# Adding the probabilities of two key blocks before the product with ones

## The reference, cut to what matters

```python
q = (xn @ Wq)  # 8 heads of 32;  k, v: 2 key heads, each shared by 4 query heads
scores = where(causal, rope(q) @ rope(k).T * scale, NEG);   out = softmax(scores) @ v
geo = where(causal, qp[:, None] * kp[None, :], NEG);         geo_out = softmax(geo) @ v
out = out + head_scales * (geo_out - out);   attention = out @ Wo
z = xn @ ternary(W_syn).T + b_syn;  keep the 102 largest of 1024 per row, relu
ffn = layernorm(xn + hidden @ ternary(W_out).T + b_out)
```

## Time and profile before

| | |
|---|---|
| median of 3 runs | 785.38 us (783.82 to 786.79) |
| the profiled execution | 785.15 us, of which the span is 783.4 us |
| mean granted TensorE clock | 0.896 |
| busy in the span | PE 703.4, DVE 495.6, ACT 464.9, POOL 262.5 us |

### The profile page before, as it was taken

How to read it: one execution, slowest core, us unless ns; L and a number is a source line. 1 busy time by engine, 2 the same in 40 slices (tenths; PEclk the granted TensorE clock), 3 DMA queues, 4 the chain that set the end, 5 groups by cost and what they waited for, 6 DMA issues and landing times. The chain is left out here.

```text
span 783.4 us, 12828 instructions
## 1 busy us (share of the span) xinstructions
PE 703.4 (90%) x4536; PEld 351.5 (45%) x4536; DVE 495.6 (63%) x1022; ACT 464.9 (59%) x789; POOL 262.5 (34%) x390
## 2 busy tenths in 40 slices
PE   2779889989999997999999997799999999989954
PEld 1445434455344344543344334544544455554434
DVE  3798498854675686266474648274575576856463
ACT  3354762058654611765554461688889888988930
POOL 5516562043214104331030102302433543343355
PEclk9876987589799975999999898899999999999986
DMA  8100000000000000000000000000000000000000
GB/s 234 63 1 4 7 2 7 0 3 1 1 8 1 1 1 2 1 5 6 1 1 1 1 2 1 10 1 8 8 8 8 8 8 15 8 8 8 2 0 28
DMA packets 12373, 9.41 MB, mean 12 GB/s; under 512 B 5713, under 2 KB 11729, under 8 KB 12306
## 3 DMA queue, kind: packets, MB, share of 16 engines
q1 hardware_dynamic: 12306, 8.55, 3.8%
HBM read 5.80 MB, written 2.10 MB: 10 GB/s over the span
## 5 line engine op out<-in xcount | busy, mean ns | idle before, releaser
L728 ACT ACTIVATE probs<-scores 128x1024 f32<-128x1024 f32 (+3 forms) x320 | 269.8, 893 | 153.9 <-PE acc L1208 56.3
L1208 PE MATMUL acc<-probs,v_nat 128*32 128x512 f32 (+3 forms) x1280 | 159.0, 570 | 6.1 <-POOL probs L606 5.8
L1208 PE MATMUL acc<-probs,ones_all 128*32 128x512 f32 (+3 forms) x1280 | 153.7, 553 | 0.0
L926 DVE TENSOR_REDUCE piece_max<-side 128x1 f32<-128x512 f32 x156 | 103.5, 686 | 73.9 <-PE side L1107 72.9
L606 POOL TENSOR_SCALAR_AFFINE_SELECT probs<-probs 128x256 f32<-128x256 f32 x128 | 57.9, 463 | 156.8 <-ACT probs L728 155.8
L1107 PE MATMUL side<-k_stack,q_stack 96*128 96x512 f32 (+3 forms) x232 | 93.5, 462 | 3.7 <-DVE piece_max L926 1.8
L1188 PE MATMUL scores<-q_stack,k_stack 98*128 98x512 f32 (+3 forms) x320 | 92.2, 398 | 2.4 <-ACT probs L728 2.4
L1208 PEld LDWEIGHTS acc<-probs,ones_all 128*32 128x32 f32 x1280 | 43.0, 115 | 82.9 <-issue 80.1
L1107 PEld LDWEIGHTS side<-k_stack,q_stack 96*128 96x128 f32 x232 | 42.1, 203 | 71.2 <-issue 45.6
L1188 PEld LDWEIGHTS scores<-q_stack,k_stack 98*128 98x128 f32 x320 | 55.3, 195 | 27.5 <-ACT probs L728 19.1
L641 POOL TENSOR_TENSOR xb<-xn,b_down 128x256 f32<-128x256 f32 x16 | 12.4, 776 | 147.8 <-DVE y_mv L1059 138.3
(11 more groups left out here) (144 smaller groups left out, 1105.9 us busy)
## 6 DMA issues: line engine op xcount, KB each, us to landing
res<-in_L_attn_x_dram SPq DMA_DIRECT2D x4, 512.0 KB, 9.2
out_dram<-res SPq DMA_DIRECT2D x16, 128.0 KB, 1.7
z_buf<-in_L_ffn_W_syn_dram SPq DMA_DIRECT2D x1, 1024.0 KB, 7.8
z_buf<-in_L_ffn_W_out_dram SPq DMA_DIRECT2D x1, 1024.0 KB, 4.9
k_geo<-geo_rows SPq DMA_DIRECT2D x24, 8.0 KB
q_geo<-geo_rows SPq DMA_DIRECT2D x24, 8.0 KB
w_qkv<-in_L_attn_Wq_dram SPq DMA_DIRECT2D x1, 256.0 KB, 4.4
tables<-in_cos_table_dram SPq DMA_DIRECT2D x1, 256.0 KB, 4.5
```

What stands on the lines that cost most here:

```text
L728: nc.scalar.activation(probs[:, slot % 2, pair, :, off:], scores[:, pair, :, off:], ACT.Exp, scale=ATT_SCALE if kind == 0 else 1.0).then_i ...
L926: free(nc.vector.tensor_reduce(piece_max[:, h, p:p + 1], pt, AX.X, ALU.max), ("S",) + a)
L1208: last = nc.tensor.matmul(acc[D * h:D * h + D, part, off:], lhs, probs[:, slot % 2, h // 2, h % 2, off:], start=first, stop=end)
```

## The change

1. The step `vs` is parted in two: `val` (the product with `v_nat`, every slot) and `sum` (the product with ones, every second slot).
2. Before a `sum`, the probabilities of the odd block j are added in place onto those of the even block j-1: pair 0 by DVE, pair 1 by POOL, one `tensor_tensor` of up to 128x1024 each (`add`). An add waits for `exp` (or `cut`) of its pair of block j and for `val` of block j-1. The columns that block j doesn't have stay as they were in j-1.
3. `probs` gets three buffers, and the planner chooses which one an `exp` takes: that of an even block is free after its `sum`, that of an odd block after its `val` and both adds.
4. Each copy after a pass waits only for its own half of `acc`, and each half of `acc` only for its own copy.
5. To make room, `z_buf` goes from three buffers to two (`z` of tile t waits for `hide` of t-2) and `q_geo` from two to one: `geo_dma` of chunk c now waits for the last `val` of chunk c-1. The bias row `b_up` moves from the third buffer of `z_buf` into `work`, so the first `pick` waits for the bias to be split.

```diff
-            wait = [("vs", c - 2, G - 1, 1, TPC * (c - 1) - 1)] if c >= 2 else []
+            wait = [("val", c - 2, G - 1, 1, TPC * (c - 1) - 1)] if c >= 2 else []
...
-            + ([("vs", c - 2, G - 1, 1, TPC * (c - 1) - 1)] if c >= 2 else []))
+            + ([("val", c - 1, G - 1, 1, TPC * c - 1)] if c >= 1 else []))
...
-                + ([("hide", t - 3)] if t >= 3 else [("w_put", 1, 3), ("b_split",)]), empties=("z", t, half))
+                + ([("hide", t - 2)] if t >= 2 else [("w_put", 1, 3), ("b_split",)]), empties=("z", t, half))
...
-        add("vs", "pe", 13, ("vs", c, g, kind, j), 60 + 1700 * share,
-            [("cut" if j >= TPC * c else "exp", c, g, kind, j, PAIRS - 1)]
-            + ([("o_raw",) + epilogues[e - 1], ("d_raw",) + epilogues[e - 1]] if j == 0 and e else []), "columns")
+        add("val", "pe", 13, ("val", c, g, kind, j), 60 + 850 * share,
+            [(made, c, g, kind, j, PAIRS - 1)] + ([("o_raw",) + epilogues[e - 1]] if j == 0 and e else []), "columns")
+        if j % 2:
+            for pair in range(PAIRS):
+                add("add", ADDERS[pair], 0, ("add", c, g, kind, j, pair), (150 + 2340 * share) / 2 if ADDERS[pair] == "dve" else 150 + 2500 * share,
+                    [(made, c, g, kind, j, pair), ("val", c, g, kind, j - 1)])
+            add("sum", "pe", 12.5, ("sum", c, g, kind, j), 60 + 850 * min(1, share + 1 / TPC * (j >= TPC * c)),
+                [("add", c, g, kind, j, pair) for pair in range(PAIRS)]
+                + ([("d_raw",) + epilogues[e - 1]] if j == 1 and e else []), "columns")
...
+    def kept_until(i):
+        if kept[i] is None:
+            return 0.0
+        c, g, kind, j = kept[i]
+        if j % 2 == 0:
+            users = [("sum", c, g, kind, j + 1)]
+        else:
+            users = [("val", c, g, kind, j)] + [("add", c, g, kind, j, pair) for pair in range(PAIRS)]
+        return max(done[u] for u in users) + HAND if all(u in done for u in users) else None
...
+                if k == "add":
+                    c, g, kind, j, pair = a
+                    off = max(0, j - TPC * c) * P
+                    if j >= TPC * c:
+                        dve.wait_ge(cut_ready, cut_no[a] + 1)
+                    else:
+                        dve.wait_ge(probs_ready, score_no[a] + 1)
+                    dve.wait_ge(vals_used, val_no[(c, g, kind, j - 1)] + 1)
+                    even, odd = (probs[:, buffer[(c, g, kind, i)], pair, :, off:] for i in (j - 1, j))
+                    nc.vector.tensor_tensor(even, even, odd, ALU.add).then_inc(added[pair], 1)
...
-                    for part, lhs in enumerate((v_nat[:, j, g], ones[:, 0:D])):
-                        for h in range(HG):
-                            last = nc.tensor.matmul(acc[D * h:D * h + D, part, off:], lhs,
-                                                    probs[:, slot % 2, h // 2, h % 2, off:], start=first, stop=end)
-                    last.then_inc(probs_used, 1)
+                    for h in range(HG):
+                        last = nc.tensor.matmul(acc[D * h:D * h + D, 0, off:], v_nat[:, j, g],
+                                                probs[:, buffer[a], h // 2, h % 2, off:], start=(j == 0), stop=(j == TPC * (c + 1) - 1))
+                    last.then_inc(vals_used, 1)
+                if k == "sum":
+                    c, g, kind, j = a
+                    e = epi_no[a[:3]]
+                    off = max(0, j - 1 - TPC * c) * P
+                    for i in range(PAIRS):
+                        pe.wait_ge(added[i], add_no[i][a] + 1)
+                    if j == 1 and e >= 1:
+                        pe.wait_ge(d_ready, e)
+                    for h in range(HG):
+                        last = nc.tensor.matmul(acc[D * h:D * h + D, 1, off:], ones[:, 0:D],
+                                                probs[:, buffer[(c, g, kind, j - 1)], h // 2, h % 2, off:],
+                                                start=(j == 1), stop=(j == TPC * (c + 1) - 1))
+                    last.then_inc(sums_used, 1)
```

More of the change, by code:

```diff
@@ L147, in build_plan @@
         share = 1 - max(0, j - TPC * c) / TPC
+        e = epilogues.index((c, g, kind))
+        made = "cut" if j >= TPC * c else "exp"
         for pair in range(PAIRS):
@@ L238, in build_plan @@
                 ready = max(ready, min(free_from(i) for i in spare))
+            if key[0] == "exp" and key[5] == 0:
+                spare = [kept_until(i) for i in range(BUFFERS) if kept_until(i) is not None]
+                if not spare:
+                    continue
+                ready = max(ready, min(spare))
             if key[0] == "score":
@@ L259, in build_plan @@
                     holds[BANKS + 2 * key[5] + i] = key
+        if key[0] == "exp" and key[5] == 0:
+            i = min((i for i in range(BUFFERS) if kept_until(i) is not None), key=kept_until)
+            earlier[key[1:5]], kept[i] = kept[i], key[1:5]
+            buffer[key[1:5]] = i
         clock[eng] = start + ns
@@ L426, in attention_and_ternary_ffn @@
         cut_ready = sem("cut_ready")
-        probs_used = sem("probs_used")
-        raw_ready = sem("raw_ready")
+        vals_used = sem("vals_used")
+        sums_used = sem("sums_used")
+        added = [sem(f"added{pair}") for pair in range(PAIRS)]
+        o_ready = sem("o_ready")
+        d_ready = sem("d_ready")
         recip_ready = sem("recip_ready")
@@ L722, in _ @@
                     off = max(0, j - TPC * c) * P
-                    slot = slot_no[(c, g, kind, j)]
                     act.wait_ge(score_full, n + 1)
-                    if pair == 0 and slot >= 2:
-                        act.wait_ge(probs_used, slot - 1)
-                    nc.scalar.activation(probs[:, slot % 2, pair, :, off:], scores[:, pair, :, off:], ACT.Exp,
+                    last = earlier[a[:4]]
+                    if pair == 0 and last and last[3] % 2 == 0:
+                        act.wait_ge(sums_used, sum_no[last[:3] + (last[3] + 1,)] + 1)
+                    if pair == 0 and last and last[3] % 2 == 1:
+                        act.wait_ge(vals_used, val_no[last] + 1)
+                        for i in range(PAIRS):
+                            act.wait_ge(added[i], add_no[i][last] + 1)
+                    nc.scalar.activation(probs[:, buffer[a[:4]], pair, :, off:], scores[:, pair, :, off:], ACT.Exp,
                                          scale=ATT_SCALE if kind == 0 else 1.0).then_inc(probs_ready, 1)
@@ L1192, in _ @@
                             last = nc.tensor.matmul(dst[:, off:], k_geo[rows, P * j:P * j + P],
-                                                    q_geo[rows, b, g, off:], start=True, stop=True)
+                                                    q_geo[rows, g, off:], start=True, stop=True)
                     last.then_inc(score_full, 1)
-                if k == "vs":
+                if k == "val":
                     c, g, kind, j = a
-                    slot, e = slot_no[a], epi_no[a[:3]]
+                    e = epi_no[a[:3]]
                     off = max(0, j - TPC * c) * P
-                    first, end = j == 0, j == TPC * (c + 1) - 1
                     if j >= TPC * c:
```

91 lines of the change are left out of this document (54 added, 37 removed).

## The result

The changed kernel takes 850.03 us (median of 4 runs, 847.88 to 876.3) where the kernel before takes 785.38: the ratio is 1.0815, with a 95% interval of 1.0782 to 1.0847. It is slower by 65 us, where 32 us of gain were forecast. The profiled execution has a span of 848.4 us.

A forecast was written before the change was run, and what follows sets the result against it. PE was taken to bound C and most of B, and D with ACT close behind; DVE set A's second half. Gains of 1 + 8.7 + 14.4 + 8 = 32 us from 785.15 gave 753 us, range 728 to 789.

The forecast's parts named there:

- the waits: PE waits 0.25 us per sum for adds: 2, 4, 6, 8 us in A to D; exp's buffer waits 0.
- the room: Fewer buffers: q_geo and the bias cost 0; for z_buf only 8 of the 17 us that ACT allows in D were taken.
- PE's time: Ones products removed take 66.0 us from PE: 5.1, 12.7, 20.4 and 27.8 in A to D.
- A: Stretch 58 to 165 us, from chunk 0's row-maxima transfer to chunk 1's; DVE ends it; gain put at 1 us.
- D: Stretch 492 to 760 us, from chunk 3's row-maxima transfer; ACT's limit 251 us; gain put at 8 us.
- B: Stretch 165 to 304 us, from chunk 1's row-maxima transfer to chunk 2's; gain put at 8.7 us.
- C: Stretch 304 to 492 us, from chunk 2's row-maxima transfer to chunk 3's; PE sets the pace; gain put at 14.4 us.
- the adds: A full add takes 1.25 us on DVE, 2.35 on POOL; neither engine passes its stretch, hidden beside PE in B, C, D.
- contention: DVE and POOL block each other when both read two operands from SBUF; cost put inside the 0.25 us per sum.
- the path shared by DVE and POOL: Rival: this path bounds D, which gives 0, while B gives 3 and C 6: 776 us, chance 0.25.
- the named point of decision: Time from z to hide of 35.4 us, allowed by two z_buf buffers; from there the third rival decides.
- third rival: Two z_buf buffers space FFN tiles 20.0 us instead of 17.7, costing 33 us in D or behind attention: 794 us, chance 0.18.

The follow-up runs named there:

- b_half: Kernel before, order and waits untouched, with the ones product left out for odd key blocks (denominators wrong): 753.69 us, ratio 0.9602.
- b_z2: Kernel before with two z_buf buffers instead of three and the bias in work, no adds: 825.28 us, ratio 1.0511.
- a_onecol: Changed kernel, same order and waits, with each add on one column only (denominators wrong): 808.8 us, two executions.
- b_z2_half: Kernel before with both two z_buf buffers and the ones products of odd blocks left out: 790.91 us, ratio 1.0089.
- a_pool1: Changed kernel in its order, POOL's adds on one column, DVE's whole (denominators wrong): 822.75 us, ratio 1.0503.
- a_exp_z3: Changed kernel with exp rank 1.5 instead of 0 and a third z_buf buffer laid on the rope tables: 810.26 us, ratio 1.0288.
- a_exp_z3_pool1: a_exp_z3 in its order with POOL's adds on one column, DVE's whole (denominators wrong): 761.98 us, ratio 0.9686.
- split3: Changed kernel without adds: whole ones product, val and sum every slot, three probs buffers, one q_geo, third z_buf on the rope tables: 761.48 us, ratio 0.9701 to before.
- split3_b2: split3 with two probs buffers instead of three, order planned anew: 789.28 us, ratio 1.0047 to the kernel before.
- a_dve1: Changed kernel in its order, DVE's adds on one column, POOL's whole (denominators wrong): 830.7 us, two executions, ratio 1.0585.
- a_both_pool: Changed kernel with both adds on POOL and none on DVE, order planned anew: 839.2 us, ratio 1.0689.
- b_q1: Kernel before with one q_geo buffer instead of two, nothing else: 785.09 us, ratio 0.9991.
- a_exp: Changed kernel with the planner's rank of exp 1.5 instead of 0, so that z goes first: 818.9 us, ratio 1.0358.
- a_one_exp_z3: a_one_plan_z3 with exp rank 1.5 instead of 0: 745.1 us from two of four executions, which spread up to 776.7.
- a_one_plan_z3: Changed kernel with one-column adds, planned at 100 ns each, and three z_buf buffers, inputs left out for room (output wrong): 794.58 us, ratio 1.0128.
- a_rank6: Changed kernel with the planner's rank of the adds 6 instead of 0: 847.43 us, ratio 1.0797.
- a_z3: Changed kernel with three z_buf buffers again, room made by leaving out inputs, order planned anew: 860.16 us, ratio 1.0997.

## Why the prediction was wrong

The account: PE's saving -31 (b_half), the lost `z_buf` buffer +40 (b_z2), the new order +18 (a_onecol less b_z2_half), the adds' own time +41 (after less a_onecol). That is +68, against 65 measured. In the forecast's terms the saving was 53 (3, 12.7, 20.4 and ACT's 17), the waits took 12 of it and `z_buf` 9, which leaves 32; measured are 31, 41 + 18 and 40. The steps that failed are the waits, at 12 for 59 us, the room, at 9 for 40, and the size of the saving. The first two terms of the account are measured each alone and together. The 18 and the 41 hold for these orders; with lag and room mended POOL's adds alone cost 48. In a schedule in which several chains wait for each other, such terms depend on what is mended first, and the account is one way to cut the loss, not the only one.

**1, PE's time: mis-sized.** The instructions went as counted: the ones product fell from 153.7 to 83.6 us busy, foretold "some 85". But 66 us of PE are worth 31 us of time. A gave 0 (the sum had 1), and D stopped at ACT's bound (251.8 us, foretold 251). B and C gave 6 and 13 of 12.7 and 20.4. In both PE's busy time fell by less (8 and 14 us) than what was counted, and PE kept its gaps (9 us of B, 7 of C). The instructions on `acc` in C of b_half:

```profile
297.70:472.70 175.00, 68.00 (x576) 14.15 (x576) 4.47 (x8) 0.93 0.01 2
```

They lost 17.6 us (85.64 before), not 20.4, and those on `scores` took 2.9 more in exchange (46.0 to 48.9). So PE was the bound of C, where the time fell with the busy time, 13.3 for 13.6; but the mean busy time of a product was more than its removal gave.

**2, the adds: sizes right, hidden wrong.** POOL's shortest full add took 2.34 us (2.35 foretold), DVE's 1.16 (1.25). Their means are 2.88 and 1.48, their longest 3.45 and 3.41. That none passes its stretch's length was true, and no argument: POOL, busy for half of B and C and two thirds of D, is not the bound of any stretch, and its adds are yet 27 of 41 us (a_pool1), or 48 us by themselves (a_exp_z3 less a_exp_z3_pool1). What counts is the latency from the value product to POOL's end, with the other chains of POOL ahead of it.

**3, the waits: the step that failed most.** `sum` waited 23.1 us for POOL and 4.5 for DVE, where 80 x 0.25 = 20 had been put in, so the named wait was about right. "The two against each other at 0" was wrong twice. ACT stood 68.7 us for the odd block's buffer, because POOL's add reads it last; ACT's waits for a buffer grew from 56 to 99 us. And the third buffer is not small change: without adds it is worth 28 us (split3 against split3_b2). The change gives the buffer and takes it back, since an odd block now stays for its value product and then for a slow add, and an even one until the `sum` behind the next. The granted clock of C fell below 0.94, to 0.91, the sign that the prediction had named for gaps that cost more than their length; its sum has no term for it, and no run prices it.

**4, contention.** The lock is in the trace again: L699 beside DVE's add takes 1.59 us where its like L696 takes 0.72, and ends 0.58 after DVE's 1.25 us are over. The Trainium skill's "SBUF — State Buffer", section "Who interferes with whom", says that such a pair shuts each other out; the rows agree. As a bound of the whole ("the path shared by DVE and POOL") it falls: a_pool1 and a_dve1 take 27 and 19 us of 41, not each the whole, and with no adds on DVE (a_both_pool, replanned) only 11 us come back. By the means over the shortest, full-size adds stood 48 x 0.54 = 26 us longer on POOL and 48 x 0.32 = 15 on DVE; how much of it lay on the path no run tells. The prediction's "the sum 20 us better" without the lock was wrong by its own sum: D went by ACT's limit, so the waits stood in it with 12 us (2, 4 and 6).

**5, the room.** `q_geo` at 0 was right (b_q1). `z_buf` was the edit with a price; in the forecast I took off 9 us of the 17 that ACT allowed in D, and the rival's formula gave 33 us. It measured 40, with the mechanism of the rival: two buffers, and tiles left behind the attention. In the changed kernel its sign came true, 39.2 us from `z` to `hide` and intervals of 22.7. The argument against it, tile 1's 26.3 us, was one tile in a still empty stretch; the mean of 40.1 us for `z` to `hide` stood in the same paragraph, and was over the 35.4 that was the named point of decision. I should have believed it. But the point was no sharp one: in b_z2 the time from `z` to `hide` fell to 34.3 us, and the 40 us were lost all the same, because a buffer also stands empty between `hide` and the next `z`, up to 18.9 us there.

**Not in the prediction: the lag.** The buffers of `probs` also set the pace between attention and FFN. With a third one the planner ran `exp`, of rank 0, ahead; the tail of a_onecol is 84 us where b_z2_half has 68. One rank gives 31 us back (a_exp), and some 49 in a_one_exp_z3. That the third buffer is what lets it run ahead is argued, not shown, and it can't be the buffer alone: split3 has it too, with `exp` at rank 0, and leaves no tile over; a_one_plan_z3, with as many `z_buf` buffers, leaves five, with half of the ones products gone and waits for (one-column) adds. Whether all of the 18 us is the lag stays open too: a_rank6 takes the tail away as well and gains nothing, and a_one_exp_z3 scatters by 36 us. Also open is why a_z3 is slower than after: its order differs everywhere, and no run holds that order fixed.

The forecast of 753 us happens to be the time of b_half, PE's saving with none of the prices. The third rival had the side right and a fifth of the chance; at 794 it is short by the lag and the adds. One reading of the start was careless, without weight: ACT stands at 8 in slice 10 as well.

## What to carry to other kernels

Work moved from a full engine to a half idle one isn't free where it sits between a producer and the release of its buffer: count the latency to the last reader, with the other chains of that engine ahead of it, and how long each buffer is kept. Price the room that an edit takes by its own test (here +40 and 0), and try the room without the edit: the third `probs` buffer, brought in to carry the adds, was worth 28 us without any add. And where two chains share a schedule, look at how many tiles of the slower one are left at the end, before anything else; a priority number can be worth as much as the change.

## What the hardware showed beside it

The granted clock of PE moved with the schedule, not with the work. split3 has before's 4536 products, and PE's clock in B, C and the attention of D was 0.98, 0.99 and 0.99, against 0.87, 0.94 and 0.96 before and 0.89, 0.91 and 0.93 after; over the span 0.942, 0.896 and 0.867. The sum of PE's gaps does not explain it: in B split3 has 6 us of them at 0.98 and before 7 at 0.87; in the attention of D split3_b2 has 16 at 0.98 and before 14 at 0.96. Nor is the clock what makes split3 fast. split3_b2, with the same products, had 0.933 to 0.944 in its ten executions, and PE busy for 90% of the span as before, and took 789 us. What raised the clock in these two kernels no run tells.

PE's busy time in a profile is no measure of its work either: after, with 640 products less, shows the same 703 us. So a product's busy time holds for the schedule in which it was read.
